# Registers loaded ahead and a tile's expert work spread over more steps, in a fused attention and expert kernel

## The reference, cut to what matters

```python
x = x + _L0_attn_ref(xn, ...) + _L0_ffn_ref(xn, ...)   # 4 heads, linear attention; 8 experts, top 2
xn = _layernorm(x, axis=-1)
x = x + _L1_attn_ref(xn, ...) + _L1_ffn_ref(xn, ...)   # 16 heads, softmax with ALiBi; 8 experts, top 2 of 2 groups

# experts, for each token and each of its two experts e:
u, gate = jnp.split(xn @ w_up[e].T, 2, axis=-1)
h = u * jax.nn.silu(gate)
out += weight * (h @ w_down[e].T)
```

## Time and profile before

| | |
|---|---|
| median of 3 runs | 862.86 us |
| lowest and highest run | 862.05 and 874.87 us |
| the profiled execution: its time | 857.87 us |
| the profiled execution: its span | 856.0 us |
| PE busy in the span | 661.8 us |
| granted PE clock, mean | 0.868 |

### The profile page before, as it was taken

The page is one execution under the profiler, slowest core; times in us unless marked ns, Lnnn a source line. Parts: engine busy times, 40 slices in busy tenths (PEclk is TensorE's granted clock), DMA queues, the critical chain, the costliest instruction groups (busy, mean ns, idle before and its releaser), DMA issues.

```text
span 856.0 us, 13039 instructions
## 1 busy us (share of the span) xinstructions
PE 661.8 (77%) x3695; PEld 489.2 (57%) x3695; DVE 410.8 (48%) x1540; ACT 437.5 (51%) x1184; POOL 319.1 (37%) x281
## 2 busy tenths in 40 slices
PE   3474999722497899899978788768878888789897
PEld 3363666511265676676755566446746566556666
DVE  6553443224454538844623553354434453446464
ACT  1655444311364567666754555455554555455653
POOL 4577100044566223357852222123202321132771
PEclk9998999956566897995995999799987999789979
DMA  9412122130010000001100000000000000000131
GB/s 343 141 47 71 45 63 67 31 129 12 13 38 13 1 1 25 26 22 45 48 4 13 14 13 19 19 13 20 14 19 13 19 13 20 13 10 8 39 82 30
DMA packets 33075, 33.74 MB, mean 39 GB/s; under 512 B 4512, under 2 KB 28992, under 8 KB 32240
## 3 DMA queue, kind: packets, MB, share of 16 engines
q1 hardware_dynamic: 28912, 24.52, 9.1%
q0 software_dynamic: 4096, 8.40, 3.4%
HBM read 19.85 MB, written 13.04 MB: 38 GB/s over the span
## 4 chain that ended last, share of the span: by engine, by line
PE 36%; POOL 11%; DVE 10%; issue 10%; ACT 6%; DMA 2%; DVEq 0%; POOLq 0%; ACTq 0%
PE b_upB L1681 7%; PE b_last L1724 6%; POOL sorted_rows L511 4%; POOL rn L570 3%; PE b_upA L1388 3%; ACT prb L841 2%; PE b_rest L1705 2%; POOL taken L542 2%; PE b_upA L1645 2%; PE b_upB L1669 2%; DVE th L1276 2%; PE b_last L1388 2%; DMA taken<-expert_rows,pos 1%; PE b_last L1390 1%; PE b_last L1389 1%
## 5 line engine op out<-in xcount | busy, mean ns | idle before, releaser
L570 POOL TENSOR_TENSOR rn<-ss,halves 128x8 f32<-128x8 f32 x64 | 105.1, 1642 | 358.0 <-DVE ss L1264 349.9
L1331 DVE CUSTOM_DVE_ANT_0 prb<-b_upB,bias 128x130 f32<-128x130 f32 (+1 forms) x256 | 83.2, 357 | 169.4 <-PE b_upB L1681 168.1
L841 ACT ACTIVATE prb<-prb,mneg 128x130 f32<-128x130 f32 (+1 forms) x256 | 114.6, 449 | 84.6 <-DVE mneg L1331 84.5
L1724 PE MATMUL b_last<-v,prT 128*128 128x64 f32 x768 | 117.4, 294 | 12.9 <-DVE qs_all L1319 12.9
L1724 PEld LDWEIGHTS b_last<-v,prT 128*128 128x128 f32 x768 | 108.1, 212 | 28.5 <-DVE qs_all L1319 16.4
L1681 PE MATMUL b_upB<-qkT 64*128 64x258 f32 (+1 forms) x512 | 102.2, 432 | 3.4 <-DVE pnT L1341 1.4
L771 ACT ACTIVATE qk<-b_last 128x512 f32<-128x512 f32 x59 | 35.1, 596 | 99.0 <-PE b_last L1390 98.6
L1681 PEld LDWEIGHTS b_upB<-qkT 64*128 64x128 f32 x512 | 52.4, 220 | 46.4 <-issue 35.5
L511 POOL DMA_INDIRECT sorted_rows<-xf_all,pos x64 | 65.6, 1026 | 27.5 <-issue 18.8
L1705 PE MATMUL b_rest<-cst,prb 128*128 128x128 f32 x384 | 72.7, 302 | 1.6 <-ACT prb L841 0.9
L852 ACT ACTIVATE prT<-b_rest 128x512 f32<-128x512 f32 (+1 forms) x128 | 61.3, 479 | 18.0 <-PE b_rest L1705 15.7
(11 more groups left out here) (301 smaller groups left out, 1338.0 us busy)
## 6 DMA issues: line engine op xcount, KB each, us to landing
moe_buf<-sorted_rows SPq DMA_DIRECT2D x20, 128.0 KB, 2.5
expert_rows<-moe_buf SPq DMA_DIRECT2D x20, 128.0 KB, 1.8
moe_buf<-sorted_rows SPq DMA_DIRECT2D x39, 64.0 KB, 1.9
expert_rows<-moe_buf SPq DMA_DIRECT2D x39, 64.0 KB, 1.5
sorted_rows<-v SPq DMA_DIRECT2D x2, 1024.0 KB, 6.7
bias<-w_up SPq DMA_DIRECT2D x1, 2048.0 KB, 13.1
down<-w_dn SPq DMA_DIRECT2D x2, 1024.0 KB, 9.5
moe_buf<-w_up SPq DMA_DIRECT2D x4, 512.0 KB, 4.0
```

The costliest lines, as they stand in the source:

```text
L570: nc.gpsimd.tensor_tensor(rn[hs], ss[hs], halves[:], ALU.pow).then_inc(*pool_f1(f"root{n}"))
L841: nc.scalar.activation(prb[p % 3][:, i, 0:n], prb[p % 3][:, i, 0:n], ACT.Exp, scale=-1.0, bias=mneg[:, qt, h:h + 1], accum_out=lsum[:, qt, ...
L1331: nc.vector.tensor_tensor_reduce(prb[p % 3][:, i, 0:n], b_sim[i][:, 0:n], bias[:, h, KEYS - n:KEYS], 1.0, FMAX, ALU.add, ALU.min, mneg[:, ...
L1724: ins = nc.tensor.matmul(b_pv[:, at:at + DH1], prT[p3 % 3][:, i, c * P:(c + 1) * P], v[:, c, h * DH1:(h + 1) * DH1], start=(p3 % 4 == 0 an ...
```

## The change

Two things change.

First, expert numbers are loaded into registers ahead, once instead of twice. In the pair stage `load_experts(s + 1)` stands behind the up products of pair `s`; the up and the down products of a pair use the same two registers. For the tiles `load_expert(i + 1)` stands behind the up product of tile `i`; the first is loaded at late 0 of tile 0.

Second, a tile's work is spread over more steps. The up product goes from late 0 to late 1, Tanh and DVE's two products from 1 to 2, the transposes from 1 to 3, ACT's copy and the down product from 2 to 4, DVE's copy out from 3 to 5. Turning and splitting the rows stays at late 0. Since `late` decides the parity of the step, the up product and the transposes (of the tile before) now share an even step `p`, and the turn and the down product an odd one, beside the projections. Within `tile_matmuls` the order becomes transposes, up, down.

```diff
             def tile_gate(b, p):
-                for i in tile_at(b, p, 1):
+                for i in tile_at(b, p, 2):
...
-                for i in tile_at(b, p, 2):
+                for i in tile_at(b, p, 4):
...
             def tile_hidden(b, p):
-                for i in tile_at(b, p, 1):
+                for i in tile_at(b, p, 2):
...
             def tile_rows(b, p):
-                for i in tile_at(b, p, 3):
+                for i in tile_at(b, p, 5):
...
+            pair_experts = {}
+
+            def load_experts(s):
+                if s < PAIRS:
+                    pair_experts[s] = [pe.value_load(slot_expert[0][0:1, 2 * s + t:2 * s + t + 1], min_val=0, max_val=E - 1) for t in range(2)]
+
             def pair_ups(s):
...
-                for t in range(2):
-                    e = pe.value_load(slot_expert[0][0:1, 2 * s + t:2 * s + t + 1], min_val=0, max_val=E - 1)
+                for t, e in enumerate(pair_experts[s]):
...
                 ins.then_inc(pair_pe["up"], 1)
+                load_experts(s + 1)
...
-                for t in range(2):
-                    e = pe.value_load(slot_expert[0][0:1, 2 * s + t:2 * s + t + 1], min_val=0, max_val=E - 1)
+                for t, e in enumerate(pair_experts.pop(s)):
...
             pe.wait_ge(*ROUTED("slots"))
+            load_experts(0)
...
             def tile_matmuls(b, p):
-                for i in tile_at(b, p, 2):
-
-                    pe.wait_ge(tile_act["hidT"], i + 1)
-                    if i == 0:
-                        pe.wait_ge(dn1_in, 16)
-                    e = tile_expert(i)
...
                 for i in tile_at(b, p, 0):
                     if i == 0:
-                        pe.wait_ge(up_lo[1], 4)
                         pe.wait_ge(*ROUTED("slots", 1))
-                    else:
-                        pe.wait_ge(tile_dve["hid"], i)
-                    pe.wait_ge(tile_dve["xl"], i + 1)
-                    e = tile_expert(i)
...
-                for i in tile_at(b, p, 1):
+                        load_expert(0)
+                for i in tile_at(b, p, 3):
...
+                for i in tile_at(b, p, 1):
+
+                    if i == 0:
+                        pe.wait_ge(up_lo[1], 4)
+                    else:
+                        pe.wait_ge(tile_dve["hid"], i)
+                    pe.wait_ge(tile_dve["xl"], i + 1)
+                    e = tile_experts[i]
...
+                    load_expert(i + 1)
+                for i in tile_at(b, p, 4):
+
+                    pe.wait_ge(tile_act["hidT"], i + 1)
+                    if i == 0:
+                        pe.wait_ge(dn1_in, 16)
+                    e = tile_experts.pop(i)
```

More of the change, by code:

```diff
@@ L1610, in tile_turn, with load_expert @@
                     nc.tensor.transpose(b_tile, tile_in[i % 4], ident).then_inc(tile_pe["turn"], 1)
-            def tile_expert(i):
-                return pe.value_load(slot_expert[1][0:1, i:i + 1], min_val=0, max_val=E - 1)
+            tile_experts = {}
+            def load_expert(i):
+                if i < TILES1:
+                    tile_experts[i] = pe.value_load(slot_expert[1][0:1, i:i + 1], min_val=0, max_val=E - 1)
             def tile_matmuls(b, p):
-                for i in tile_at(b, p, 2):
-                    pe.wait_ge(tile_act["hidT"], i + 1)
-                    if i == 0:
-                        pe.wait_ge(dn1_in, 16)
-                    e = tile_expert(i)
-                    for a in range(HB):
-                        ins = nc.tensor.matmul(b_up[:, 0:D], tile_hidT[i % 2][:, a],
-                                               down[:, bass.ds(e, 1), a * D:(a + 1) * D].rearrange("p e n -> p (e n)"),
-                                               start=(a == 0), stop=(a == HB - 1), skip_group_check=True)
-                    ins.then_inc(tile_pe["down"], 1)
                 for i in tile_at(b, p, 0):
                     if i == 0:
-                        pe.wait_ge(up_lo[1], 4)
                         pe.wait_ge(*ROUTED("slots", 1))
-                    else:
-                        pe.wait_ge(tile_dve["hid"], i)
-                    pe.wait_ge(tile_dve["xl"], i + 1)
-                    e = tile_expert(i)
-                    mine = slice(i % 2 * P, (i % 2 + 1) * P)
-                    matmul3(b_gate, xf_h[:, mine], xf_l[:, mine], up_h[:, bass.ds(e, 1), :].rearrange("p e n -> p (e n)"),
-                            up_l[:, bass.ds(e, 1), :].rearrange("p e n -> p (e n)")).then_inc(tile_pe["up"], 1)
-                for i in tile_at(b, p, 1):
+                        load_expert(0)
+                for i in tile_at(b, p, 3):
                     pe.wait_ge(tile_dve["hid"], i + 1)
@@ L1646, in tile_matmuls @@
                     ins.then_inc(tile_pe["hidT"], 1)
+                for i in tile_at(b, p, 1):
[5 more added lines that the diff above has]
+                    e = tile_experts[i]
+                    mine = slice(i % 2 * P, (i % 2 + 1) * P)
+                    matmul3(b_gate, xf_h[:, mine], xf_l[:, mine], up_h[:, bass.ds(e, 1), :].rearrange("p e n -> p (e n)"),
+                            up_l[:, bass.ds(e, 1), :].rearrange("p e n -> p (e n)")).then_inc(tile_pe["up"], 1)
+                    load_expert(i + 1)
[4 more added lines that the diff above has]
+                    e = tile_experts.pop(i)
+                    for a in range(HB):
+                        ins = nc.tensor.matmul(b_up[:, 0:D], tile_hidT[i % 2][:, a],
+                                               down[:, bass.ds(e, 1), a * D:(a + 1) * D].rearrange("p e n -> p (e n)"),
+                                               start=(a == 0), stop=(a == HB - 1), skip_group_check=True)
+                    ins.then_inc(tile_pe["down"], 1)
             def scores(b, p):
```

## The result

The median went from 862.45 us (4 runs, 859.59 to 874.87) to 733.31 us (4 runs, 728.49 to 735.02). The ratio is 0.850, 95% interval 0.845 to 0.856. The profiled execution's span went from 856.0 to 731.5 us, 124.5 us less.

The account below looks back on a forecast made before the run. PE was taken to be held by waits ahead of tile matmuls and by load holes in the pairs; 8 us (pairs) plus 41 (tiles) made 49 off, giving 809 from the profiled execution or 814 from the median; predicted 812, range 784 to 838.

Parts of the forecast that it names:

- new waits (a) to (e): Tile stage: ACT's order (up to 0.37 us a tile), copy out, up product's bank, SP's loads, last tile; costed at nothing.
- additive: Tile stage, upper price: a tile costs all its array time on top of a tile-free round; 25 us gained.
- only the load's hole stays: Tile stage, lower price: of 68.7 us of waits only 0.3 us for each of 39 tiles remains; 57 us gained.
- What comes back: Tile stage: PE waits more for the attention's own chain, at most about 2.2 us a tile with the slower clock.
- The yardstick of 62.6 us: Tile stage: the mean of tile-free rounds 1 and 2 (64.4 and 60.7 us), to which tile costs were added.
- a hole of 0.3 us a tile that stays: Tile stage: the load behind the up product leaves PE a hole of 0 to 0.45 us, taken as 0.3.
- the prediction's own formula: Clock: a stage at mean clock c costs about 1 + 1.2 x (1 - c) times its full-clock time.
- rival 3: Tile stage: waits close and the clock rises as well, 82 us off, about 780 us; chance 0.10.
- The four holes: Pair stage: PE holes behind freshly loaded expert numbers, together 0.85 us a pair, close with the numbers in registers.
- The new hole of 0.45 us: Pair stage: two loads in a row open a hole behind the up products, 0.2 to 1.2 us, taken as 0.45.
- The sequencer goes ahead of the array: Pair stage: the sequencer needs at most 0.5 us for a group on which the array spends 0.80.
- The loss that the prediction worked out from it: Pair stage: with the page's 600 ns load, a hole of about 1.05 us and a loss of some 4 us.

Follow-up runs that it names:

- E7: Changed kernel with the tile's transposes, ACT's copy, down product and copy out one step earlier: 829.3 us, rounds 3 to 6 303.6 us.
- E3: Kernel before with only the tiles' work spread over more steps in the new order, numbers loaded at each use: 829.6 us, ratio 0.900.
- E11: Changed kernel with two unused loads more for each tile: 812.9 us (one run), rounds 3 to 6 280.9 us.
- E4: Kernel before with the whole tile change, pair stage left as before: 810.8 us, ratio 0.880, rounds 3 to 6 259.3 us.
- E16: Kernel before with four useless matmuls ahead of each of a tile's two waits: 861.4 us against 863.0, ratio 1.000.
- E8: Changed kernel with three unused 512-column matmuls in every even step of rounds 2 and 7: 786.0 us.
- E15: Changed kernel again, unchanged, on the chip of the load-check runs: 732.3 us, ratio 0.851 to the kernel before.
- E6: Kernel before with the pairs' numbers loaded one pair ahead, but four loads a pair: 914.4 us (one run), a pair 4.24 us.
- E10: Kernel before with the pairs' numbers loaded one pair ahead, three loads a pair: 907.4 us (one run), a pair 3.61 us.

## Why the prediction was right or wrong

The direction was right, and so was the mechanism of the tile stage; its size was not. 129 us came off where 51 were forecast, and 733 us lies below the range's 784. The bound of the pair stage was missed. Step by step:

**The bound of the tile stage: right.** Every PE wait named in the earlier trace rows stood ahead of a tile's group, and with these waits the time went. None of the new waits (a) to (e) appeared: the largest wait left is 3.3 us for ACT's copy, and the expected ones for probabilities or scores come to 0.8. PE idles 5.8 us where 15 to 40 were forecast.

**The price of the tile stage: the step that failed most, 41 us forecast, 104 measured.** The forecast took the middle between "additive" (25 us) and "only the load's hole stays" (57). Three of its terms were wrong, in one direction.

- "What comes back", the attention's chain waited for more. The tiles' array time was to cost up to 1.73 us on top of a tile-free round, 2.2 with the slower clock. Against the one tile-free round at full clock, 60.3 us in E7, round 4 with its 66.6 us adds 6.3, or 0.57 us a tile. Most of the tiles' array time fell into times in which PE idles otherwise: 9.2 us in that round, 1.3 in round 4. The yardstick of 62.6 us was flawed besides. It held 17 and 20 us at the lower clock in rounds 1 and 2, and the length of round 2 doesn't follow PE's clock.
- The lower price was taken from named waits, 68.7 us, of which 64 came off. That idle time isn't the whole loss. By starts each of the two holes in the earlier trace rows is 0.16 to 0.19 us longer than the idle time named (1.46 and 1.49 against 1.30), since the end of the group ahead counts as busy. And a group behind a hole lasts longer: four down matmuls ahead of the projections take 0.37 us to the next group in E3, and 0.46 where PE idled just before them (medians of 16 and 14). For 78 holes these two come to some 20 us, an estimate. The prediction had the price by starts in its hands, 7.90 - 4.95 = 2.95 us a tile or 115 us, and called it the most that can come off.
- Loads: forecast as a hole of 0.3 us a tile that stays. E11 prices two superfluous ones at 0.55 us a tile, and E3 against E4 shows 13 us, 0.33 us a tile, gained by the tiles' loads being once and ahead. The hole didn't stay.

**The clock: a missed term.** It was held at 0.90 and put at nothing, and became 1.00, outside the 0.85 to 0.95 that the prediction itself had named as a sign of being wrong. E16 shows that holes in those places keep it down. By the estimate above this is 16 to 19 us; the prediction's own formula, with 12% for a clock of 0.90, would have made it 39 of 364. The Trainium skill, TensorE: Matmul & The Clock Gate, section HAM oscillation, has idle stretches between groups of matmuls throw PE to half rate; the stretches of its case are waits for DMA, longer than the holes here. The trace agrees in rounds 3 to 6 (0.90, 0.99 in E16, 1.00 after), and in rounds 0 to 2 and round 2 of E8 it doesn't account for what is seen. The forecast took the low clock of rounds 1 and 2 as evidence against the rule in all rounds. But those rounds have no low clock of their own (1.00 in round 1 of E7, 0.94 in round 2 of E15), and their small idle time goes with it. Its own rival 3, "waits close and the clock rises", named what happened, with 0.10 chance and 82 us of gain for 129.

**The pair stage: forecast 8 us, measured 24.** The four holes were seen and their closing was right. Two steps failed. The new hole of 0.45 us behind two loads didn't open: the sequencer's two loads fit just beside 1.5 us of up products. And the array's own need was put at 4.19 - 0.85 = 3.34 us; it is 2.95. It was read from groups that stood apart, and the transposes from twice a group of two: two up products 2 x 0.80, now 111.11 - 110.33 = 0.78 and 111.81 - 111.11 = 0.70; eight down matmuls 1.08, now 112.92 - 112.03 = 0.89; four transposes 0.44, now 0.36. "The sequencer goes ahead of the array" was taken from one moment (120.5) and not summed over the pair: 4 x 0.63 = 2.5 of 4.1 us. The prediction's own 0.75 us from a load to its first product, four times, was 3.0 of 4.19, and could have named the bound. The Trainium skill, DMA: Bandwidth & Descriptors, section Latency and other measured facts, puts a floor of about 600 ns on such a load. The instruction lasts 296 ns here, so the row stood against it; as the whole cost to the sequencer, 0.63 us by E6 and E10, the page's figure is close. The loss that the prediction worked out from it did not come: it set the figure in place of the 0.30 alone and kept the load's gaps on top, and 0.63 us is measured with the gaps in it.

**The rest: right.** No DMA came into the way, round 7 stayed at about 50 us, and half as many loads stand in the trace.

## What to carry to other kernels

Sum what the sequencer of an engine has to do over one period of a loop (loads of registers, checks, address work), and not only where a hole shows. It is in no busy time and can be the bound: then moving a load helps little (the period changed by 0.2 us at most here) and removing one gives its whole cost until the array is the bound. Where an in-order engine waits twice in a period for results that it asked for in the same period, price both waits together, and by starts: here more came off than the named idle time, since holes are longer by starts, groups behind them run longer, and the clock fell. As the yardstick of a stage without holes, take one at the same clock, and one whose length is set by the same engine.

## What the hardware showed that was not expected

- A load of one number into a register costs PE's sequencer 0.63 us in this loop (4.24 and 3.61 us with four and three), twice the 0.296 us of the load instruction. Its place made little difference (4.1 us behind the waits, 4.12 to 4.21 ahead of them, 4.24 a pair ahead).
- Leaving out a load's bounds moved the range check to each use, and made a pair 0.6 to 0.8 us longer.
- The clock of one stage differs between executions of the same kernel. Round 2 had 20 us at the lower clock in one profile of the changed kernel and 7 in another (E15), and lasted 60.6 us in both, so PE's clock doesn't set it. In round 1 each us at the lower clock cost about 0.25 us (60.3 us with none, 67.2 with 27). Three more long matmuls in every second step (E8) left the clock of round 2 at 0.81. What takes the clock down in rounds 0 to 2 stays open.
- Eight filler matmuls for each tile, put into the holes, raised the clock from 0.90 to 0.99 and left the time the same (ratio 1.000, 0.996 to 1.004): what the clock gave, the fillers took.
